# Routing work of a fused vision tower in four pieces, rows normalised on ScalarE, and ScalarE's copies ahead of the exponentials

## The reference

```python
h = tokens(x)                                  # patch projection, class token, * pos_embed
h = h + attention0(layernorm(h))               # top-64 mask, three powers of the attention
h = h + moe0(layernorm(h))                     # 64 experts, 2 chosen, capacity 128
h = h + attention1(layernorm(h))
h = h + moe1(layernorm(h))
# attention1: q, k, v and t from layernorm(h) @ W_qkv, 8 heads of 64;
#   out = per head [softmax(q k^T / 8) v , dist t] @ W_out + b_out, dist a fixed 65x65 matrix
# moe1: logits, idx = top_k(x @ gate_w + gate_b, 2), weights = softmax(logits) (8 experts)
#   h_e = relu(x @ w1[e] + b1[e]);  out = sum over the 2 chosen of weight * (h_e @ w2[e] + b2[e])
```

## Time and profile before

| | us |
|---|---|
| median of 3 runs (1911.02 to 1920.24) | 1911.95 |
| the profiled execution | 1911.31 |
| its span, first to last instruction | 1909.5 |
| TensorE busy in the span | 1680.6 (88%) |
| VectorE busy | 1083.4 (57%) |
| ScalarE busy | 844.3 (44%) |
| GpSimd busy | 828.7 (43%) |
| mean granted TensorE clock | 0.953 |

### The profile page before, as it was taken

How to read it: one execution, slowest core, us unless ns; L and a number is a source line. 1 busy time by engine, 2 the same in 40 slices (tenths; PEclk the granted TensorE clock), 3 DMA queues, 4 the chain that set the end, 5 groups by cost and what they waited for, 6 DMA issues and landing times. The chain is left out here.

```text
span 1909.5 us, 61793 instructions
## 1 busy us (share of the span) xinstructions
PE 1680.6 (88%) x24177; PEld 1240.5 (65%) x24177; DVE 1083.4 (57%) x3322; ACT 844.3 (44%) x2304; POOL 828.7 (43%) x990
## 2 busy tenths in 40 slices
PE   8999997899999998887999979888888888539997
PEld 3444444677677766664877557777777777439997
DVE  0000016887787777755666545565665556627774
ACT  0000025655655555535444545554454445226652
POOL 0000002787777777760011023456455464724444
PEclk9999998999999999998699989999999999769999
DMA  9877710000000000003000000000000000024422
GB/s 379 325 307 289 307 65 1 4 3 3 3 3 3 3 3 3 3 3 99 1 1 1 1 2 2 8 19 19 19 13 22 16 18 19 29 65 128 128 78 59
DMA packets 47216, 117.18 MB, mean 61 GB/s; under 512 B 10731, under 2 KB 29470, under 8 KB 46972
## 3 DMA queue, kind: packets, MB, share of 16 engines
q1 hardware_dynamic: 39198, 99.25, 14.4%
q0 software_dynamic: 6096, 12.94, 1.9%
q10 hardware_dynamic: 1678, 1.43, 0.2%
HBM read 96.80 MB, written 18.61 MB: 60 GB/s over the span
## 5 line engine op out<-in xcount | busy, mean ns | idle before, releaser
L1339 PE MATMUL ps<-xn,s_a_wqkv 128*128 128x260 f32 x1024 | 295.3, 413 | 68.4 <-ACT qk_a L780 60.6
L170 PE MATMUL ps<-x_chunk,s_w_tok 128*128 128x512 f32 x576 | 252.0, 599 | 6.2 <-DMA x_chunk<-in_x_main 6.2
L1339 PEld LDWEIGHTS ps<-xn,s_a_wqkv 128*128 128x128 f32 x1024 | 177.6, 194 | 118.7 <-ACT qk_a L780 79.9
L170 PEld LDWEIGHTS ps<-x_chunk,s_w_tok 128*128 128x128 f32 x576 | 109.8, 192 | 147.1 <-issue 147.1
L939 ACT ACTIVATE e_a<-e_a 128x585 f32<-128x585 f32 (+1 forms) x128 | 85.2, 665 | 241.9 <-DVE e_a L1233 147.4
L197 DVE SCALAR_TENSOR_TENSOR h<-ps,s_b_tok,s_pos 128x512 f32 (+1 forms) x16 | 11.3, 746 | 249.3 <-PE ps L178 249.3
L612 POOL MEMSET cls_queries_a<- 128x1040 f32 x2 | 1.9, 966 | 345.9 <-POOLq L221 345.9
L1224 DVE TENSOR_REDUCE neg_max_a<-ps 128x8 f32<-128x520 f32 x128 | 89.3, 698 | 108.1 <-PE ps L1317 108.1
L1423 PE MATMUL ps<-s_a_wqkv,xn_pair_a 128*64 128x256 f32 x1024 | 138.4, 389 | 5.2 <-ACT weightsT_m L887 2.8
L1966 POOL DMA_INDIRECT out<-block_out_m,block_m x93 | 92.1, 990 | 113.7 <-DVE block_out_m L2069 106.0
L736 POOL TENSOR_TENSOR prob_a<-e_a,inv_sum_a 128x512 f32<-128x512 f32 x64 | 66.8, 1043 | 167.4 <-DVE inv_sum_a L1267 88.3
(11 more groups left out here) (283 smaller groups left out, 4392.8 us busy)
## 6 DMA issues: line engine op xcount, KB each, us to landing
x_chunk<-in_x_main SPq DMA_DIRECT2D x96, 768.0 KB, 8.5
block_m<-pair_rows SPq DMA_DIRECT2D x93, 130.0 KB, 2.1
pair_rows<-pad_rows_m SPq DMA_DIRECT2D x29, 130.0 KB
s_f_all<-in_f_w SPq DMA_DIRECT2D x2, 1024.0 KB
x_ends<-in_x_tail SPq DMA_DIRECT2D x16, 96.0 KB, 10.7
out<-block_out_m,block_m POOLq DMA_INDIRECT x93
s_w_tok<-in_w_tok SPq DMA_DIRECT2D x6, 192.0 KB, 6.7
pair_rows<-rows_m,slot_i_m POOLq DMA_INDIRECT x65, 2.5
```

The costliest lines, as they stand in the source:

```text
L170: last = nc.tensor.matmul(ps[:, bank, :], w_tok[:, k, :], xb[:, s, k, :], start=(k == 0), stop=False)
L1339: nc.tensor.matmul(ps[:, QK_BANK[i], 0:QUAD], w_qkv[:, c * P:(c + 1) * P], xn[:, t.h * QUAD:(t.h + 1) * QUAD], start=True, stop=True).then ...
```

## The change

1. ScalarE's step takes the values and the first copy of queries or keys ahead of the exponentials.
2. `normalise_rows` moves from GpSimd (j=0) to ScalarE (j=1, behind the copy of the ranks), as one activation a tile, row * rstd + shift. VectorE makes shift = -mean * rstd in `find_best`, one more instruction.
3. `choose` is cut: what follows the chosen pair moves to a new `weigh_choices` in j=1. `measure_rows` takes two tiles in j=1 and the rest in j=2, where `find_moments` follows.
4. `send` stores two tiles in j=1, one in j=2, the last in j=3.

```diff
-            def normalise_rows(t):
-
-                if (at := batch(t, 3)) is None:
-                    return
-                k, par = at
-                upto(pool, rstd_done, k + 1, route.batches)
-                upto(pool, sent[par], (16 * route.BATCH // 2) * (k - par), 16 * TM * route.batches)
-                pool.sem_inc(pool_waited)
-                for i in range(route.size(k)):
-                    last = nc.gpsimd.tensor_scalar(rows[:, par, i, 0:D], turned[:, par, i, 0:D],
-                                                   moments[:, par, i, 0:1], rstd[:, par, i:i + 1],
-                                                   ALU.subtract, ALU.mult)
-                last.then_inc(x_rows, 1)
...
-                if route and t.j % 4 == 0:
-                    normalise_rows(t)
                 if route and t.j % 4 == 1:
-                    send(t, 0)
+                    send(t, 0, 2)
                 if route and t.j % 4 == 2:
-                    send(t, 1)
+                    send(t, 2, 3)
+                if route and t.j % 4 == 3:
+                    send(t, 3, None)
...
+            def normalise_rows(t):
+
+                if (at := batch(t, 3)) is None:
+                    return
+                k, par = at
+                upto(act, shift_done, k + 1, route.batches)
+                upto(act, sent[par], (16 * route.BATCH // 2) * (k - par), 16 * TM * route.batches)
+                for i in range(route.size(k)):
+                    last = nc.scalar.activation(rows[:, par, i, 0:D], turned[:, par, i, 0:D], ACT.Identity,
+                                                scale=rstd[:, par, i:i + 1], bias=shift[:, par, i:i + 1])
+                last.then_inc(x_rows, 1)
...
@@ -951,14 +952,14 @@
                 else:
                     product_out(t, 0)
                     product_out(t, 1)
+                    values_out(t)
+                    qk_out(t, 0)
                     exps(t)
-                    values_out(t)
                     if route and t.j % 4 == 0:
                         exp_gaps(t)
                     if route and t.j % 4 == 3:
                         deviations(t)
                     cls_probs_out(t)
-                    qk_out(t, 0)
                     qk_out(t, 1)
                     dist_out(t)
...
-            def measure_rows(t):
...
-                    upto(dve, turned_sb, 2 * k + 2, 2 * route.batches)
+                    upto(dve, turned_sb, 2 * k + half + 1, 2 * route.batches)
                 dve.sem_inc(dve_waited)
-                for i in range(n):
+                for i in range(2 * half, n if half else 2):
                     last = nc.vector.bn_stats(stats[:, i, :], turned[:, par, i, 0:D])
...
-                upto(dve, stats_done, k + 1, route.batches)
+
+            def find_moments(t):
...
+                upto(dve, stats_done, 2 * k + 2, 2 * route.batches)
-                for i in range(n):
+                for i in range(route.size(k)):
                     last = nc.vector.bn_aggr(moments[:, par, i, :], stats[:, i, :])
                 last.then_inc(moments_done, 1)
...
+                nc.vector.scalar_tensor_tensor(out=shift[:, par, 0:n], in0=moments[:, par, 0:n, 0], scalar=-1.0,
+                                               in1=rstd[:, par, 0:n], op0=ALU.mult, op1=ALU.mult)\
+                    .then_inc(shift_done, 1)
...
-                after(t, summed)
-                first_w = chained(nc.vector.reciprocal(w01[:, 0:n, 0], wsum[:, 0:n]))
...
-                after(t, first_w)
-                second_w = chained(nc.vector.tensor_tensor(w01[:, 0:n, 1], eg[:, 0:n], w01[:, 0:n, 0], ALU.mult))
+                after(t, summed)
+                chained(nc.vector.reciprocal(w01[:, 0:n, 0], wsum[:, 0:n]))
...
-                is_low = chained(nc.vector.tensor_tensor(first_low[:, 0:n], idf[:, 0:n, 0], idf[:, 0:n, 1], ALU.is_lt))
-                after(t, second_w)
-                gapped = chained(nc.vector.tensor_tensor(diff[:, 0:n], w01[:, 0:n, 0], w01[:, 0:n, 1], ALU.subtract))
+                chained(nc.vector.tensor_tensor(first_low[:, 0:n], idf[:, 0:n, 0], idf[:, 0:n, 1], ALU.is_lt))
...
+
+            def weigh_choices(t):
...
+                after(t, done[0])
+                second_w = chained(nc.vector.tensor_tensor(w01[:, 0:n, 1], eg[:, 0:n], w01[:, 0:n, 0], ALU.mult))
                 each = chained(nc.vector.tensor_tensor(eq[:, 0:n], ids(0, E1, [P, n, 2, E1], (1, 1), route.expert_ids),
                                                        idf[:, 0:n].unsqueeze(3).to_broadcast([P, n, 2, E1]),
                                                        ALU.is_equal))
-                after(t, max(gapped, is_low))
-                scaled = chained(nc.vector.tensor_tensor(diff_low[:, 0:n], diff[:, 0:n], first_low[:, 0:n], ALU.mult))
+                after(t, second_w)
+                gapped = chained(nc.vector.tensor_tensor(diff[:, 0:n], w01[:, 0:n, 0], w01[:, 0:n, 1], ALU.subtract))
                 after(t, each)
                 weighed = chained(nc.vector.tensor_tensor(wk[:, 0:n], eq[:, 0:n], w01[:, 0:n].unsqueeze(3)
                                                           .to_broadcast([P, n, 2, E1]), ALU.mult))
+                after(t, gapped)
+                scaled = chained(nc.vector.tensor_tensor(diff_low[:, 0:n], diff[:, 0:n], first_low[:, 0:n], ALU.mult))
+                after(t, weighed)
+                upto(dve, wtt_ps, k, route.batches)
+                nc.vector.tensor_tensor(wt[:, 0:n], wk[:, 0:n, 0, :], wk[:, 0:n, 1, :], ALU.add).then_inc(wt_done, 1)
                 upto(dve, sent[par], (16 * route.BATCH // 2) * (k - par), 16 * TM * route.batches)
                 nc.vector.tensor_copy(rows[:, par, 0:n, NAME:NAME + 1].rearrange("p t o -> p (t o)").bitcast(I32),
                                       names[:, bass.ds(k * route.BATCH, n)])
                 after(t, scaled)
                 nc.vector.tensor_tensor(rows[:, par, 0:n, W_LO], w01[:, 0:n, 1], diff_low[:, 0:n], ALU.add)
                 nc.vector.tensor_tensor(rows[:, par, 0:n, W_HI], w01[:, 0:n, 0], diff_low[:, 0:n], ALU.subtract)
-                after(t, weighed)
-                upto(dve, wtt_ps, k, route.batches)
-                nc.vector.tensor_tensor(wt[:, 0:n], wk[:, 0:n, 0, :],
-                                        wk[:, 0:n, 1, :], ALU.add).then_inc(wt_done, 1)
...
                 if route and t.j % 4 == 0:
                     choose(t)
+                if route and t.j % 4 == 1:
+                    weigh_choices(t)
+                    measure_rows(t, 0)
                 if route and t.j % 4 == 2:
-                    measure_rows(t)
+                    measure_rows(t, 1)
+                    find_moments(t)
                     seat(t)
                 if route and t.j % 4 == 3:
                     find_best(t)
```

19 lines of the change are left out of this document (15 added, 4 removed).

## The result

The changed kernel took 1852.91 us (median of 4 runs, 1847.98 to 1861.77), the kernel before 1912.11 us: a ratio of 0.9687, interval 0.9636 to 0.9737. In a second session it was 1849.15 us (6 runs) against 1908.84, ratio 0.9696 (0.9674 to 0.9719). The forecast was 1853 us. The profiled execution took 1857.18 us (span 1855.4), some 4 us above the median.

What follows compares the result with a forecast made beforehand. TensorE bounds the kernel, losing time to waits for ScalarE's copies and a lower clock. Waits 40.5 and 1.5 us, slow stretches 15.0, drain 1.6, together 58.6: 1911.3 becomes 1852.7, said as 1853; range 1836 to 1881.

Steps and rivals of the forecast that it cites:

- The wait moves to the fourth projection and is shorter: Odd steps of attention 1: TensorE's wait moves one projection on, leaving 0.4 us in j=1, 0.85 in j=3; 40.5 us gained.
- VectorE's relief in j=3: Second odd step of a group: two statistics leave j=2, so the differences of j=3 end 0.43 us earlier.
- The parts' shares: Odd steps: ScalarE's order alone gains 0.85 us each; VectorE's pieces free 1.2 us ahead of j=1, 0.43 ahead of j=3.
- the plain sum of the four: Whole kernel, chance of faster: forecast 0.56, A 0.12, B 0.18, C 0.08; given as 0.94, said to be a little less.
- The slow stretches hang on waits of 1.9 us and more: Attention 1 beside routing: nine lower-clock stretches follow waits of 1.91 us or more; shorter waits remove them, 15.0 us.
- C: Rival, attention 1: slow stretches stay, hanging on load over longer time and not on these waits; 1868 us, chance 0.08.
- Rows on ScalarE: End of j=1: four row activations take 1.0 us (bounds 0.8 to 3.2), covered by ScalarE's 1.06 us wait; nothing on the path.
- B: Rival, odd steps: the wait mostly moves to the next projection, half the slow stretches go; 34 us gained, 1877 us, chance 0.18.
- E: Rival, pairs of steps: slower, the probability chain takes over and TensorE waits for GpSimd's probabilities; 1918 us, chance 0.03.
- The drain: 1.6 us gained: End of the stage: GpSimd's row multiplies go, but the last addition waits for the biases; 1.6 us gained (0 to 4).
- A: Rival, attention 1: TensorE waits no more at all, 16.0 us more go; 1837 us, chance 0.12.

## Why the prediction was right

The forecast was 1853 us and the mechanism was the one written down. That the sum came out within a microsecond or two is in part luck, as the second point tells. Its steps, with what the runs make of each:

- **The wait moves to the fourth projection and is shorter.** Right: 21.3 us in 27 waits, where 15 to 20 in some 25 were said. In j=1 it is 0.35 and 0.52 us (said 0.4). In j=3 it is 1.18 to 1.27 (said 0.85). The step that was mis-sized is VectorE's relief in j=3, where 0.43 us were taken off. From the copy of the transposed probabilities of j=2 to the maxima of j=3 VectorE took 4.07 to 4.11 us before, 3.76 to 3.84 with its pieces alone, and 3.91 to 3.98 in the changed kernel: 0.14 us. The two statistics bring 0.38 us, but others among what stays grew, here before and after:

```profile
1306.69 0.24 DVE L1141 TENSOR_TENSOR place_m<-ranks_m,next_row_m 128x112 f32<-128x112 f32 x1
...
1307.68 0.22 DVE L1150 CAST slot_i_m<-slot_f_m 128x4 int32<-128x4 f32 x1
```

```profile
1319.44 0.42 DVE L1156 TENSOR_TENSOR place_m<-ranks_m,next_row_m 128x112 f32<-128x112 f32 x1
...
1320.61 0.54 DVE L1165 CAST slot_i_m<-slot_f_m 128x4 int32<-128x4 f32 x1
```

And TensorE comes 0.36 us earlier through the even step, where the prediction counted only the wait of 0.15, so it waits longer for the same VectorE. In the changed kernel ScalarE needs 1.49 us from the start of the exponentials to TensorE's next start (1322.30 to 1323.79), just the 1.5 that the prediction had; it is their start that is late.
- **The parts' shares.** ScalarE's order alone was priced at 0.85 us an odd step and brought 0.5 to 0.6; VectorE's pieces at 1.2 and 0.43, and brought 1.0 and 0.25. All were read some 0.2 to 0.3 us too high: 42.0 us of waits were to go, and 38.3 went (59.6 to 21.3). The length of the whole group came out right all the same, 29.6 forecast against 29.6 and 29.9, because a group without its waits, 28.4 us before (32.80 less 4.42), is 28.1 now (29.75 less 1.67). No step had forecast that; over 13 groups it is some 4 us, and it covers what the waits fell short by. The chance given for faster, 0.94, is the plain sum of the four, with nothing taken off.
- **The slow stretches hang on waits of 1.9 us and more.** Right, and now shown in both directions: shorter waits by three ways took them away (ScalarE's order, VectorE's pieces, both), longer waits, made by needless copies, brought them back. The limit in these groups is a little lower than thought: behind waits of 1.84 to 1.86 us four came, three of them without ScalarE's order and one with the rows alone. C (1868 us) falls. Eight of the nine lie in the twelve groups of the kernel before; its four groups without one have 32.7 us in the mean, and the eight are 13.8 us longer than eight of those, 1.7 each as said. All nine stretches are then 15.5 us, where 15.0 were said.
- **Do the parts add up?** Over twelve groups ScalarE's order took off 35.6 us and VectorE's pieces 28.7, the rows added 3.7. The first two both hold the 13.8 us of slow stretches, which go only once: 35.6 + 28.7 - 13.8 = 50.5. The rows add 2.0 without their extra slow stretch: 48.5. The whole change took off 50.2.
- **Rows on ScalarE.** Nothing on the path in the groups, as said, but not for the price said: 1.64 us for four and 0.48 for each, where 1.0 and under 0.3 were taken from the copy's 290 ns. Between the bounds of 0.8 and 3.2 it lies in the middle. The cover was short by 0.6 us, and the slack of the even step took that. Rivals B (1877) and E (1918) fall with it: no odd wait over 1.3 us, and TensorE didn't wait for GpSimd's probabilities in any group.
- **The drain: 1.6 us gained.** Within its range of 0 to 4, as far as can be told. From the last fourth projection, which stands behind the last odd wait in both kernels, to the last indirect store it was 60.6 us before, 60.5 in one profile of the changed kernel and 57.3 in the other. The step overlooked that ScalarE's rows stand ahead of the output copies there, and TensorE waits 2.28 us for these, where it waited 0.88. TensorE, ScalarE and GpSimd in the drain:

```profile
1583.04 1.08 PE L1475 MATMUL ps<-s_ident,prob_a 128*128 128x128 f32 x4 [2.28 <-ACT resT_a L780]
```

```profile
1580.71 1.64 ACT L885 ACTIVATE rows_m<-turned_m,row_shift_m,row_rstd_m 128x128 f32<-128x128 f32 x4
1582.24 0.65 ACT L780 ACTIVATE resT_a<-ps 128x260 f32<-128x260 f32 x2
```

```profile
1614.74 1.53 POOL L637 TENSOR_TENSOR rows_m<-rows_m,turned_m 128x640 f32<-128x640 f32 x1 [2.76 <-ACT rows_m L897]
```

The last addition waits for the biases, as the prediction has it, 2.76 us long. The two profiles differ by the clock above all (windows from the last transpose of the choice weights in the twelve groups to the last store, changed kernel, first and second profile):

```profile
1555.56:1622.26 66.70, 40.76 (x486) 33.86 (x484) 41.10 (x193) 22.27 (x68) 34.27 (x40) 0.68 0.10 35
```

```profile
1554.03:1617.56 63.53, 36.94 (x486) 30.69 (x484) 41.02 (x193) 22.28 (x68) 34.34 (x40) 0.76 0.11 37
```

The kernel before had 0.75 in the same stretch, so the second, with 0.76, is the one to set beside it: 3.2 us gained. One profile of each isn't enough to say more.

- **A and the rest of the wait.** TensorE didn't stop waiting, but it could: with all three copies ahead the stage has no such wait left, and 1821 us are reached, below the 1837 of A, since the group then is 27.6 us and not 28.3.

What stays open is the pause at the scores of j=2: 0.7 to 0.85 us with the rows in j=3, 0.6 to 0.85 with the deviations later, 1.1 to 1.2 with two copies ahead, 0.2 to 0.45 with three needless copies. It is in every group of these four kernels and in no group of the other nine; the four differ from the changed kernel only in ScalarE's instructions, and in the first of them TensorE's rows up to the pause agree to 0.01 us with the changed kernel, which hasn't got it. That GpSimd's indirect stores are issued just ahead of it was the one idea that I tried, and the kernel chosen for it had no pause to begin with. The cause isn't known.

## What to carry over

Read, for each copy that empties a bank, what stands ahead of it in its engine's queue: a copy that needs only TensorE should not stand behind an exponential that needs VectorE. When one is moved ahead, the wait goes to the next copy in the queue, so move all that TensorE takes next (here three) before the gain is counted. With two of three nothing was gained, in part because the third copy held TensorE for 0.72 us a group, in part because of the unexplained pause of 1.1 us; with three it was 28 us. And price a wait with what follows it: here waits of 1.84 us and more in the groups also cost 1.7 us of lower clock, now and then, which the shorter ones there don't.

## What the hardware showed

- In the groups with routing, where TensorE is else some 90% busy, a wait of 1.84 to 2.55 us can be followed by a stretch at the 1.2 GHz level (clock 0.57 over 4 us), and none followed a wait of 1.83 us or less there in any of these kernels. It is not each time: of 12 waits of 2.12 to 2.19 us in one kernel 7 had one, and of eight waits of 1.84 and 1.85 us three. Nor does the longer wait have it more often: in the kernel before, nine waits of 2.06 to 2.09 us in j=1 had it once, the twelve of 1.91 to 1.99 us eight times.
- Elsewhere it also came behind shorter waits: in attention 0 behind two (1.65 and 1.72 us) of the 19 waits of over 1.5 us in all profiles together, and in the drain of the changed kernel behind one of 1.75 us. So 1.84 us is what these groups show and no rule for other streams.
- A 128x128 activation from and to SBUF with a scale and a bias for each partition takes 0.48 us on ScalarE, and several overlap to 0.40 or 0.41 each (1.64 us for four, 2.02 for five); GpSimd took 0.80 for the same.
- Freeing GpSimd moves its other work. In the changed kernel the gate bias, which ran beside the probability multiply at a median of 1030 ns, is clear of it:

```profile
L1080 DVE TENSOR_TENSOR logit_m<-logit_m,s_f_gate_b x16: 191/192/201, 1177.6 to 1604.6; 128x32 f32<-128x32 f32 x15, 128x40 f32<-128x40 f32 x1
```

while with the rows alone moved a 128x4 minimum took 0.39 us for 0.18, beside GpSimd's pair copy.
- TensorE can stand still once in each group for 0.2 to 1.2 us with no semaphore to wait for, with four of ScalarE's programs and not with nine others; TensorE's own program is the same in all.
